# Selective scan on one core: multiplying by B and scanning two states per VectorE instruction instead of one

## The reference, cut to what matters

```python
def step(h, inp):
    dt, bt, ct, ut = inp
    h = jnp.exp(dt[..., None] * A) * h + (dt * ut)[..., None] * bt[:, None, :]
    return (h, jnp.einsum('bdn,bn->bd', h, ct))
...
dts = jnp.einsum('kbrl,kdr->kbdl', dt_stack, dt_w)
delta = jax.nn.softplus(dts + dt_b[:, None, :, None])
A = -jnp.exp(A_logs)
ys = jax.vmap(_selective_scan)(xs, delta, A, Bst, Cst, Ds)
y = ys.sum(0)
```

## Time and profile before

| | us |
|---|---|
| median of 3 runs | 269.21 (268.89 to 273.89) |
| the profiled execution | 269.08 |
| its span, first to last instruction | 267.3 |
| DVE busy | 196.7 (74%) |
| PE busy | 231.5 (87%) |
| POOL busy | 126.6 (47%) |
| ACT busy | 139.4 (52%) |
| first `times_b` start to last scan end | 30.89 to 150.61 |

### The profile page before, as it was taken

One profiled execution on the slowest core, in us unless ns is written; L12 is line 12 of the kernel. 1 busy time (PEld: TensorE's weight loads), 2 busy tenths in 40 slices (PEclk: granted clock), 3 DMA queues, 4 the chain that ended last, 5 costly groups with the idle time before them and its releaser, 6 DMA issues.

```text
span 267.3 us, 2866 instructions
## 1 busy us (share of the span) xinstructions
PE 231.5 (87%) x738; PEld 97.5 (36%) x738; DVE 196.7 (74%) x291; ACT 139.4 (52%) x202; POOL 126.6 (47%) x121
## 2 busy tenths in 40 slices
PE   7989769899698986998998754997999999999992
PEld 2423233223232322322222232554654454545530
DVE  5405999999999999999999586177585464463543
ACT  4147985767576763766666820133633333433430
POOL 5612665777477763777777895996000000000000
PEclk9999968999979997999999996559999999999999
DMA  5699000000000000000000019700000903600000
GB/s 156 147 204 202 9 1 1 2 1 0 0 0 0 0 0 0 2 1 0 0 0 1 1 38 229 154 0 0 0 1 2 259 3 104 159 0 0 0 0 20
DMA packets 8292, 11.35 MB, mean 42 GB/s; under 512 B 6678, under 2 KB 7255, under 8 KB 7512
## 3 DMA queue, kind: packets, MB, share of 16 engines
q1 hardware_dynamic: 8280, 11.21, 18.1%
HBM read 8.29 MB, written 0.13 MB: 31 GB/s over the span
## 4 chain that ended last, share of the span: by engine, by line
PE 33%; DVE 11%; issue 3%; POOL 3%; ACT 1%; DVEq 0%; POOLq 0%
PE ps L1002 16%; PE ps L1018 9%; POOL rings L369 3%; DVE tn L690 2%; PE ps L812 2%; DVE rings L629 2%; DVE ps L622 1%; PE ps L949 1%; DVE dm L684 1%; DVE t L719 1%; DVE gl L795 1%; PE ps L957 1%; PE ps L975 1%; PE ps L1025 1%; PE ps L941 1%
## 5 line engine op out<-in xcount | busy, mean ns | idle before, releaser
L369 POOL TENSOR_TENSOR rings<-rings 128x512 f32<-128x512 f32 x64 | 82.2, 1294 | 38.3 <-DVE rings L629 32.5
L867 PE MATMUL ps<-rings,ident 128*128 128x512 f32 x128 | 74.2, 663 | 11.9 <-POOL rings L369 11.6
L629 DVE TENSOR_TENSOR_SCAN rings<-rings,ps 128x512 f32<-128x512 f32 x64 | 76.1, 1207 | 0.2 <-ACT rings L468 0.2
L795 DVE TENSOR_TENSOR gl<-ps,si 128x512 f32<-128x512 f32 (+1 forms) x44 | 30.4, 691 | 32.7 <-ACT si L529 32.5
L468 ACT ACTIVATE rings<-delta,a_neg 128x510 f32<-128x510 f32 x64 | 44.8, 714 | 16.4 <-DVE rings L629 16.4
L529 ACT ACTIVATE si<-ps 128x512 f32<-128x512 f32 (+1 forms) x44 | 26.2, 598 | 40.7 <-PE ps L1002 39.6
L622 DVE TENSOR_TENSOR ps<-ps,du 128x512 f32<-128x512 f32 x64 | 41.9, 678 | 0.0
L476 ACT ACTIVATE rings<-ps 128x1024 f32<-128x1024 f32 x32 | 32.7, 1021 | 17.3 <-POOL rings L369 17.3
L867 PEld LDWEIGHTS ps<-rings,ident 128*128 128x128 f32 x128 | 21.5, 198 | 43.9 <-POOL rings L369 41.9
L1002 PE MATMUL ps<-fh,wup 128*128 128x512 f32 (+1 forms) x88 | 30.3, 426 | 0.7 <-DVE gl L795 0.7
L879 PE MATMUL ps<-bc,sel_row 96*128 96x512 bf16 x64 | 25.2, 397 | 3.1 <-DVE rings L629 2.7
(11 more groups left out here) (170 smaller groups left out, 195.8 us busy)
## 6 DMA issues: line engine op xcount, KB each, us to landing
wraw<-w_up_dram SPq DMA_DIRECT2D x8, 682.0 KB, 7.5
wup<-rings SPq DMA_DIRECT2D x2, 1364.0 KB, 6.6
wdn<-w_down_dram SPq DMA_DIRECT2D x4, 160.0 KB
w_conv<-conv_w_dram SPq DMA_DIRECT2D x1, 576.0 KB, 4.7
wdn<-w_down_dram SPq DMA_DIRECT2D x4, 128.0 KB
xg<-x_grp_dram SPq DMA_DIRECT2D x1, 128.0 KB, 2.8
xc<-x_chan_dram SPq DMA_DIRECT2D x1, 128.0 KB, 2.9
xt<-x_tok_dram SPq DMA_DIRECT2D x1, 128.0 KB, 2.1
```

What stands on the lines that cost most here:

```text
L369: nc.gpsimd.tensor_tensor(hc[:, q], hs[:, q], cs[:, q], ALU.mult).then_inc(weighted, 1)
L629: nc.vector.tensor_tensor_scan(hs[:, q, :], da[:, q].rearrange("p b l -> p (b l)"), driven(q), 0.0, ALU.mult, ALU.add).then_inc(scanned, 1)
L795: nc.vector.tensor_tensor(gl[0:rows, S % 4, :], ps[0:rows, BANK_H + 2 * (S % 3) + 1, :], si[0:rows, S % 2, :], ALU.mult).then_inc(glu_read ...
L867: nc.tensor.matmul(ps[:, BANK_Y, :], ident[:], hc[:, q % BODY, :], start=False, stop=last_state).then_inc(y_ready if last_state else summe ...
```

## The change

`times_b` and `scan` take two states at once. `times_b(p)` is one multiplication of 128 x 1024 over two adjacent banks, with `du` read twice; `scan(p)` is one scan over 128 x 1024 (a zero in `da` at the first token of each image starts each sequence anew). The B banks become 0, 1, 2, 3, and the projection and flip bank moves from 2 to 7, the first dt bank from 7 to 2. `b_used` and `scanned` count pairs. The DVE order becomes b0, b1, s0, s1 with a part of `prepare` after each. PE waits for a scan ahead of the even B matmuls only; POOL and ACT likewise.

```diff
-        def driven(q):
-            return ps[:, BANKS_IN[q], :]
+        def driven(p):
+            return ps[:, BANK_B + 2 * p:BANK_B + 2 * p + 2, :]
...
-        BANK_B, BANK_XP, BANK_C, BANK_Y = 0, 2, 4, 6
-        BANKS_DT = (7, 3, 4, 6)
+        BANK_B, BANK_XP, BANK_C, BANK_Y = 0, 7, 4, 6
+        BANKS_DT = (2, 3, 4, 6)
...
 # POOL
-                    wait(pool, scanned, n + 1)
                     if q % 2 == 0:
+                        wait(pool, scanned, k * N // 2 + BODY // 2 * i + q // 2 + 1)
                         wait(pool, c_kept, k * N // 2 + BODY // 2 * i + q // 2 + 1)
...
 # ACT
-                    wait(act, scanned, n - BODY + 1)
+                    if q % 2 == 0:
+                        wait(act, scanned, k * N // 2 + BODY // 2 * i + q // 2 - BODY // 2 + 1)
...
 # DVE
+                def times_b(p):
+                    g = k * N // 2 + BODY // 2 * i + p
+                    dve.wait_ge(b_ready, 2 * g + 2)
+                    nc.vector.tensor_tensor(driven(p), driven(p),
+                                            du[:, k % 2, :].unsqueeze(1).broadcast_to([D, 2, T]), ALU.mult).then_inc(b_used, 1)
+                def scan(p):
+                    g = k * N // 2 + BODY // 2 * i + p
+                    two = slice(2 * p, 2 * p + 2)
+                    dve.wait_ge(da_ready, 2 * g + 2)
+                    dve.wait_ge(b_used, g + 1)
+                    wait(dve, weighted, 2 * g + 2 - BODY)
+                    nc.vector.tensor_tensor_scan(flat(hs[:, two, :]), da[:, two].rearrange("p q b l -> p (q b l)"),
+                                                 flat(driven(p)), 0.0, ALU.mult, ALU.add).then_inc(scanned, 1)
...
                 times_b(0)
-                for q in range(1, BODY):
-                    times_b(q)
-                    scan(q - 1)
-                    if marks is not None:
-                        prepare(k + 1, q - 1, marks)
-                if marks is not None:
-                    prepare(k + 1, BODY - 1, marks)
-                scan(BODY - 1)
+                prepared(0)
+                times_b(1)
+                prepared(1)
+                scan(0)
+                prepared(2)
+                scan(1)
+                prepared(3)
...
 # PE
-                    wait(pe, scanned, n - BODY + 1)
-                    nc.tensor.matmul(driven(q),
+                    if q % 2 == 0:
+                        wait(pe, scanned, k * N // 2 + BODY // 2 * i + q // 2 - BODY // 2 + 1)
+                    nc.tensor.matmul(ps[:, BANK_B + q, :],
```

More of the change, by code:

```diff
@@ L214, in hybrid_kernel, with flat @@
         block = ctx.enter_context(nc.Block())
-        def driven(q):
-            return ps[:, BANKS_IN[q], :]
+        def driven(p):
+            return ps[:, BANK_B + 2 * p:BANK_B + 2 * p + 2, :]
+        def flat(ap):
+            return ap.rearrange("p q t -> p (q t)")
         def wait(eng, s, value):
@@ L233, in states_loop @@
                 body(k, N // BODY - 1)
-        BANK_B, BANK_XP, BANK_C, BANK_Y = 0, 2, 4, 6
-        BANKS_DT = (7, 3, 4, 6)
+        BANK_B, BANK_XP, BANK_C, BANK_Y = 0, 7, 4, 6
+        BANKS_DT = (2, 3, 4, 6)
         BANKS_DTR = (5, 1)
-        BANKS_IN = (0, 1, 3, 7)
         BANK_WARM = 4
@@ L617, in body, with prepared @@
                     dve.wait_ge(du_ready, k + 1)
[L619 to L630, removed]
-                times_b(0)
-                for q in range(1, BODY):
-                    times_b(q)
-                    scan(q - 1)
-                    if marks is not None:
-                        prepare(k + 1, q - 1, marks)
-                if marks is not None:
-                    prepare(k + 1, BODY - 1, marks)
-                scan(BODY - 1)
+                def times_b(p):
[11 more added lines that the diff above has]
+                                                 flat(driven(p)), 0.0, ALU.mult, ALU.add).then_inc(scanned, 1)
+                def prepared(part):
+                    if marks is not None:
+                        prepare(k + 1, part, marks)
+                times_b(0)
+                prepared(0)
[5 more added lines that the diff above has]
+                prepared(3)
             for k in range(K):
```

## The result

The changed kernel took 327.31 us (median of 4 runs, 325.61 to 328.84), the one before 269.49 us beside it: a ratio of 1.2155, with a 95% interval of 1.2091 to 1.2218. It is slower by 58 us. 313 was forecast; the measured time lies in the range, 0.7 us under its upper end of 328. The profiled execution took 327.48 us, its span is 325.4.

A forecast was written before the change was run, and what follows sets the result against it. VectorE was taken to bound the state loop. From 269.1 us, +29.3 for the loop's new ring of waits, +1.4 at its end and +13 for TensorE's falling clock gave 313 us, range 296 to 328.

The forecast's parts named there:

- The bound before, and the slack of the chain: State loop before: VectorE bounds it; scan end to next B row takes 2.74 us, with 2.3 us of slack.
- The cost of a wide instruction: VectorE in the loop: multiplication 1.21 us, scan 2.26 us; each of 64 dropped instructions saves 0.06 us.
- The body at full clock: Four states in the loop take 8.93 us instead of 6.83, with VectorE waiting some 0.7 and 1.6 us.
- The loop at full clock: State loop with TensorE at full clock: 149.0 us against 119.7, so 29.3 us more.
- The ring alone: Rival: loop bound by scan, POOL's products, sum, B row, multiplication, without clock loss; 299.8 us in all, chance 0.20.
- The end of the loop: After the last scan POOL has two products left instead of one: 4.1 us instead of 2.65, +1.4 us.
- The clock: TensorE's clock falls in most loop bodies, about 3.5 us each: 13 us more, between bounds 0 and 26.
- the ring with a falling clock: Main case: loop bound by waits through all engines while TensorE's clock falls; 303 to 325 us, chance 0.60.
- the case with 0.14: Rival: clock falls in every loop body at full price and handovers cost more; 326 to 335 us, chance 0.14.
- dearer handovers: Loop waits of PE, POOL and ACT cost below 0.1 us per handover, four a body: 6 us, kept for the range.
- Nothing for the banks and the dropped waits: Renaming PSUM banks and fewer waits of PE, POOL and ACT in the loop were costed at nothing.
- VectorE stays the bound: Rival: VectorE still bounds the loop and the change gives its 3.8 us; 265.3 us, chance 0.04.

The follow-up runs named there:

- Both orders that restore the cover: Changed kernel with only TensorE's order rewritten (272.38 us), or only VectorE's order made multiplication, scan, multiplication, scan (275.63 us).
- reordered kernel: Changed kernel with only TensorE's order rewritten, B rows taken out from behind the sums; 272.38 us, ratio 1.0109 to the kernel before.
- VectorE's order: Changed kernel with only VectorE's instructions reordered to b0, s0, b1, s1; 275.63 us, ratio 1.0211 to the kernel before.
- single scans: Rewritten TensorE order with wide multiplications, but scans of one state with a signal each; 269.98 us, ratio 1.0017 to the kernel before.
- the two repairs: Rewritten TensorE order, wide instructions, with prepare's part 3 moved ahead of scan 1 and the last pair scanned as two; 274.1 us, ratio 1.0172.

## Why the prediction was right, and which term was too small

- **The bound before, and the slack of the chain**: right. VectorE was gapless, and 2.74 us from a scan's end to the next B row was harmless only while VectorE had other work to cover it. That was six instructions and 5.03 us (87.47 to 92.50); the five of the prediction reach only to the first multiplication, which doesn't need that row. Both orders that restore the cover take 52 to 55 of the 58 us away.
- **The cost of a wide instruction**: right. 1.231 and 2.270 us by record, for 1.21 and 2.26. The saving of 0.06 for each instruction showed as 0.05 in steady bodies.
- **The body at full clock**: 8.93 us forecast, 9.03 measured; waits 0.7 and 1.6 forecast, 0.70 and 1.50 measured. The loop at full clock: 149.0 forecast, 150.0 in the kernel that keeps TensorE busy. The ring alone was forecast at 299.8 us for the whole; that kernel took 301.9.
- **The end of the loop**: +1.4 forecast at full clock, and right: 4.08 us, +1.4, in the reordered kernel at a grant of 1.00. It was 4.66 (+2.0) in the kernel kept busy, where the grant there was 0.70, and 5.86 (+3.2) in the changed one at 0.57. So what is over the forecast goes with the clock.
- **The clock**: right in kind, too small in size. I took 13 us, the middle between 0 and 26; it was 23 in the loop, 24.7 from the first scan on, 25 for the whole (327.3 - 301.9), so near the upper bound. I had given each fall 3.5 us and let half of the falls miss or lie on work that nobody waits for. The low clock held for 68 us of the loop, some 4.2 us for each body, and cost 23/68 = 0.34 of the time that it lasted, where 0.25 was assumed. The 3.5 us were read from one fall. The trace of before had three in its loop, and the first was longer; it held through all of this window:

```profile
36.00:42.00 6.00, 5.35 (x9) 2.21 (x10) 5.93 (x7) 3.37 (x6) 3.28 (x3) 0.50 0.00 1
```

- **The sum of the misses**: the profiled execution lies 14.5 us over the forecast of 313 (the terms add up to 312.8, 14.7 under it): 10.0 from the clock in the loop, 1.0 from the ring, 3.1 from the later start, 1.8 from the end, 0.3 outside the span, and 1.5 given back behind the loop.
- **Range and chances**: the ring with a falling clock, at 303 to 325, had the 0.60. At 327.3 the number belongs to the case with 0.14, the fall in every body at its full price; its other half, dearer handovers, did not come true. The range holds the time, by 0.7 us, because it reached up to the lower edge of that case, and not because the clock's term was well sized; that this median lies inside is partly luck, since its four executions lie on both sides of the edge (325.61 to 328.84).
- **Nothing for the banks and the dropped waits**: shown for the banks (0.9989), and within the 1 us of the full-clock loop for the waits.
- **The rivals**: "VectorE stays the bound" needed B rows ahead of the sums; with that order it is what happens, and even then the kernel is at 1.011, not at the forecast 265. That rival's price was too good: it left out that TensorE still falls idle behind `prepare` (2.3 us from 106.5 in the reordered kernel), and that a pair's products come late at the end.

## What to carry to other kernels

Before two instructions are made one, ask what their separate ends released, and what has to be moved so that they can stand together: a wide instruction is a coarse signal, and it may bring work that waits ahead of work that could go. The order on the engine that refills a buffer decides whether that matters; a refill that depends on nothing late should not stand in the queue behind work that does. And here a new wait of TensorE was paid twice, once as itself (30 us) and once in the clock (23 us), once that engine had come onto the chain; dummy matmuls in the idle stretch told the two apart in one run.

## What the runs showed of the hardware

Two things were not expected. The first: a 128 x 512 fp32 `tensor_tensor` of VectorE with all operands in SBUF (in `prepare`) took 0.66 to 0.79 us or 1.63 to 1.65, with a few between (0.86 to 1.29). In the traces of the kernels before, changed, reordered, with VectorE's order, with single scans and with the two repairs, each of the long ones began while a `tensor_tensor` of POOL, also SBUF only, was 0.2 to 0.7 us old. The short ones began ahead of such an operation, near its end, or with none running, and POOL's own product that overlapped a short one took up to 1.72 us instead of 1.27. Three operations of the kernel before, with POOL's product between them:

```profile
98.58 0.67 DVE L600 TENSOR_TENSOR rd<-gl,rd 128x512 f32<-128x512 f32 x1
98.74 1.63 POOL L369 TENSOR_TENSOR rings<-rings 128x512 f32<-128x512 f32 x1 [0.68 <-DVE rings L629]
99.28 1.64 DVE L608 TENSOR_TENSOR delta<-rd,gl 128x512 f32<-128x512 f32 x1
...
100.95 0.69 DVE L611 TENSOR_TENSOR du<-delta,u 128x512 f32<-128x512 f32 x1
```

The multiplications and scans, which have an operand in PSUM, kept their 1.2 and 2.27 us beside the same products. This was seen in the traces and not tested by itself. The second: a scan that follows its own multiplication at once started 0.16 to 0.19 us later than an independent one, 1.30 to 1.33 against 1.14 us after it.
